# Two-layer graph attention on 64 graphs: softmax by pairs of graphs, division ahead of the transposes, half groups at both ends

## What is computed

```python
nx = ln(x, ln1_g, ln1_b)
q, k, v = nx @ wq + bq, nx @ wk + bk, nx @ wv + bv      # 8 heads of 32
bias = where(adj > 0, 0.1 * adj * adj, -inf)
x1 = x + softmax(q @ k.T / sqrt(32) + bias) @ v @ wo + bo
x = x1 + gelu(ln(x1, ln2_g, ln2_b) @ w1 + b1) @ w2 + b2
w = softmax(where(adj == 0, -inf, (x @ Wq) @ (x @ Wk).T / 16))
out = layer_norm(x + w @ (x @ Wv) @ Wo + bo1, gamma, beta)
```

## Time and profile before

| | us |
|---|---|
| median of 3 runs (range) | 1021.38 (1020.01 to 1025.15) |
| the profiled execution | 1021.12 |
| its span, first to last instruction | 1019.0 |
| mean granted TensorE clock | 0.981 |
| PE, DVE, ACT, POOL busy | 959.4, 616.8, 644.4, 409.3 |

### The profile page before, as it was taken

The page is one execution under the profiler, slowest core; times in us unless marked ns, Lnnn a source line. Parts: engine busy times, 40 slices in busy tenths (PEclk is TensorE's granted clock), DMA queues, the critical chain, the costliest instruction groups (busy, mean ns, idle before and its releaser), DMA issues.

```text
span 1019.0 us, 22667 instructions
## 1 busy us (share of the span) xinstructions
PE 959.4 (94%) x7512; PEld 827.0 (81%) x7512; DVE 616.8 (61%) x2460; ACT 644.4 (63%) x1890; POOL 409.3 (40%) x310
## 2 busy tenths in 40 slices
PE   4877999999999999999999999999999999999894
PEld 4755988888898888879888888989888888988783
DVE  3445567485756658575665758476674857565554
ACT  2536658576765768576665857676585767656552
POOL 3214245253444535344443525344452534442322
PEclk9868999999999999999999999999999999999998
DMA  7001001000100001000000100010010001000000
GB/s 232 22 1 32 2 12 42 12 21 21 31 21 31 21 10 41 10 21 21 31 21 10 41 10 21 21 31 21 11 41 10 21 21 31 21 1 21 2 22 21
DMA packets 32557, 26.20 MB, mean 26 GB/s; under 512 B 3984, under 2 KB 32272, under 8 KB 32528
## 3 DMA queue, kind: packets, MB, share of 16 engines
q1 hardware_dynamic: 29584, 25.83, 7.7%
q10 hardware_dynamic: 2944, 0.01, 0.2%
HBM read 17.44 MB, written 8.39 MB: 25 GB/s over the span
## 4 chain that ended last, share of the span: by engine, by line
PE 81%; DVE 7%; issue 2%; ACT 1%; POOL 0%; DVEq 0%; POOLq 0%
PE bank L255 21%; PE bank L256 18%; PE bank L257 18%; PE bank L368 5%; PE bank L392 5%; PE bank L385 3%; PE bank L359 3%; PE bank L472 3%; DVE p_s L952 2%; DVE nx L926 2%; DVE y L1043 1%; PE bank L374 1%; PE bank L324 1%; PE bank L437 1%; ACT p_s L691 0%
## 5 line engine op out<-in xcount | busy, mean ns | idle before, releaser
L691 ACT ACTIVATE p_s<-p_s,neg_max 128x128 f32<-128x128 f32 x512 | 197.9, 390 | 86.4 <-DVE neg_max L952 86.4
L255 PE MATMUL bank<-w_hi,hT_hi 128*128 128x256 f32 x512 | 150.1, 293 | 0.0
L257 PE MATMUL bank<-w_hi,hT_lo 128*128 128x256 f32 x512 | 143.8, 281 | 0.0
L256 PE MATMUL bank<-w_lo,hT_hi 128*128 128x256 f32 x512 | 143.7, 281 | 0.0
L952 DVE CUSTOM_DVE_ANT_0 p_s<-bank,bias 128x128 f32<-128x128 f32 x512 | 113.0, 285 | 47.2 <-PE bank L359 47.2
L1267 POOL COPY rwide<-rsum 128x256 f32<-128x256 f32 x64 | 25.4, 397 | 252.8 <-DVE rsum L965 252.8
L255 PE MATMUL bank<-n2T_hi,w_hi 128*128 128x512 f32 x256 | 108.7, 425 | 1.9 <-DVE n2T_lo L855 1.9
L255 PEld LDWEIGHTS bank<-w_hi,hT_hi 128*128 128x128 f32 x512 | 96.3, 188 | 5.9 <-issue 3.0
L257 PE MATMUL bank<-n2T_hi,w_lo 128*128 128x512 f32 x256 | 100.9, 394 | 0.0
L256 PE MATMUL bank<-n2T_lo,w_hi 128*128 128x512 f32 x256 | 100.9, 394 | 0.0
L714 ACT ACTIVATE bank<-bank,b_c 128x512 f32<-128x512 f32 x128 | 84.4, 660 | 24.0 <-PE bank L257 21.6
(11 more groups left out here) (159 smaller groups left out, 2420.3 us busy)
## 6 DMA issues: line engine op xcount, KB each, us to landing
xs<-in_x SPq DMA_DIRECT2D x16, 512.0 KB, 3.5
out<-y SPq DMA_DIRECT2D x15, 512.0 KB, 2.9
adj_i<-in_adj SPq DMA_DIRECT2D x16, 256.0 KB, 2.7
w_raw<-in_L_gnn_w SPq DMA_DIRECT2D x1, 1024.0 KB, 10.4
y<-in_L_gnn_w SPq DMA_DIRECT2D x1, 512.0 KB, 8.3
vo<-in_L_gnn_w SPq DMA_DIRECT2D x1, 512.0 KB, 9.3
out<-y SPq DMA_DIRECT2D x2, 256.0 KB, 2.1
x<-in_L_gnn_wk SPq DMA_DIRECT2D x1, 256.0 KB, 6.0
```

Of the source, the lines that this page charges most:

```text
L255: mm(out, a_hi, b_hi, start=first, stop=False)
L256: mm(out, a_hi, b_lo, start=False, stop=False)
L257: return mm(out, a_lo, b_hi, start=False, stop=last)
L691: last = run(p_s[:, h, :], p_s[:, h, :], ACT.Exp, scale=-1.0, bias=neg_max[:, b % 2, h:h + 1], accum_out=psum[:, b % 2, h:h + 1])
```

## The change

There are 17 groups now: 15 of four graphs, the first and the last of two (`size`, `pair0`, `graph0`, `ln0` give sizes and counts). Attention of layer 0 goes by pairs of graphs. `scores`, `attend` and `out_project` do both graphs in one go; of a pair, row block `r` of the four holds two graphs by two heads. `exps` writes to the PSUM bank the scores came from. `divided` on DVE takes the inverse of the sums and multiplies from PSUM into `p_s` ahead of the transposes. So `widen`, `rsum_transpose`, `rT_copy` and their tiles go, and `normalise` becomes a copy (`attn_copy`). `p_transpose` writes back into the four banks, and each of ACT and DVE copies two of them.

```diff
-            def scores(g, b):
-                if b == 0:
+            def scores(g, q):
+
+                if q == 0:
                     pe.wait_ge(act_k, 2 * g + 2)
                     pe.wait_ge(act_q, 2 * g + 2)
-                pe.wait_ge(dve_x1, 4 * g + b)
-                for t in range(KT):
+                pe.wait_ge(dve_x1, pair0(g) + q)
+                for place in range(4):
+                    b, t = 2 * q + place // 2, place % 2
                     for r in range(HPT):
-                        rows_r = slice(HD * r, HD * r + HD)
-                        last = mm(bank[r][:, nodes(t)], qT[rows_r, t, nodes(b)], kT[rows_r, t, nodes(b)],
+                        part = slice(HD * r, HD * r + HD)
+                        last = mm(bank[r][:, nodes(place)], qT[part, t, nodes(b)], kT[part, t, nodes(b)],
                                   start=True, stop=True, tile_position=(HD * r, 0))
                 last.then_inc(pe_s, 1)
 
...
+            def p_transpose(g, q):
+                for r in range(HPT):
+                    pe.wait_ge(dve_p, 4 * (pair0(g) + q) + r + 1)
+                    for place in range(4):
+                        last = tr(bank[r][:, nodes(place)], p_s[:, r, place, :], ident[:, :])
+                    last.then_inc(pe_pT, 1)
+
+            def attend(g, q):
+
+                pe.wait_ge(act_pT, 2 * (pair0(g) + q) + 2)
+                pe.wait_ge(dve_pT, 2 * (pair0(g) + q) + 2)
+                pe.wait_ge(act_v, pair0(g) + q + 1)
+                for place in range(4):
+                    b, t = 2 * q + place // 2, place % 2
                     for r in range(HPT):
-                        last = mm(av_area[HD * r:HD * r + HD, nodes(t)], v[:, b, HPT * t + r, :],
-                                  pT[:, HPT * t + r, :], start=True, stop=True, tile_position=(0, HD * r))
+                        last = mm(bank[av_bank][HD * r:HD * r + HD, nodes(place)], v[:, b, HPT * t + r, :],
+                                  pT[:, r, place, :], start=True, stop=True, tile_position=(0, HD * r))
                 last.then_inc(pe_av, 1)
...
+            def out_project(g, q):
+                pe.wait_ge(dve_attn, pair0(g) + q + 1)
+                for b in range(2):
+                    for t in range(KT):
+                        last = mm(bank[wo_bank][:, row(b)], avT[:, 2 * b + t, :], wo_f[:, t, :],
+                                  start=(t == 0), stop=(t == KT - 1))
                 last.then_inc(pe_wo, 1)
...
-            def p_transpose(g, b):
-                pe.wait_ge(dve_s, 8 * g + 2 * b + 2)
-                for h in range(HEADS):
-                    if h % HPT == 0:
-                        pe.wait_ge(act_p, 8 * g + 2 * b + h // HPT + 1)
-                    last = tr(bank[p_bank[h // HPT]][:, nodes(h % HPT)], p_s[:, h, :], ident[:, :])
-                last.then_inc(pe_pT, 1)
-
-            def rsum_transpose(g, b):
-                pe.wait_ge(pool_rwide, 4 * g + b + 1)
-                for t in range(KT):
-                    last = tr(rT_area[:, nodes(t)], rwide[:, HPT * t:HPT * t + HPT, :].rearrange("p h d -> p (h d)"),
-                              ident[:, :])
-                last.then_inc(pe_rT, 1)
-
...
+            def exps(g, q, r):
+
+                act.wait_ge(dve_s, 4 * (pair0(g) + q) + r + 1)
+                for place in range(4):
+                    last = run(bank[r][:, NODES * place:NODES * place + NODES], p_s[:, r, place, :], ACT.Exp, scale=-1.0,
+                               bias=neg_max[:, r, place:place + 1], accum_out=psum[:, r, place:place + 1])
+                last.then_inc(act_p, 1)
+
+            def pT_copy(g, q, r):
+                act.wait_ge(pe_pT, 4 * (pair0(g) + q) + r + 1)
+                run(pT[:, r, :, :], bank[r][:, :].rearrange("p (h n) -> p h n", h=4), ACT.Identity).then_inc(act_pT, 1)
...
+            def divided(g, q, r):
+                count = 4 * (pair0(g) + q) + r + 1
+                dve.wait_ge(act_p, count)
+                V.reciprocal(rsum[:, r, :], psum[:, r, :]).then_inc(dve_r, 1)
+                dve.wait_ge(dve_r, count)
+                V.tensor_tensor(p_s[:, r, :, :], bank[r][:, :].rearrange("p (h n) -> p h n", h=4),
+                                rsum[:, r, :, None].to_broadcast([128, 4, NODES]), ALU.mult).then_inc(dve_p, 1)
+
+            def pT_copy(g, q, r):
+                dve.wait_ge(pe_pT, 4 * (pair0(g) + q) + r + 1)
+                V.tensor_copy(pT[:, r, :, :], bank[r][:, :].rearrange("p (h n) -> p h n", h=4)).then_inc(dve_pT, 1)
+
+            def attn_copy(g, q):
+                dve.wait_ge(pe_av, pair0(g) + q + 1)
+                V.tensor_copy(avT[:, :, :], bank[av_bank][:, :].rearrange("p (h n) -> p h n", h=4)).then_inc(dve_attn, 1)
+
```

The opening: the vectors are loaded as rows of 128 and transposed by one PE instruction (`vector_columns`), w1 (in two DMAs) and w2 come after the weights of layer 1 and the broadcast rows, and ACT and DVE make the parts of w2 at the end of the first turn (`high_w2` ahead of the exponentials of group 1, `low_w2` last on DVE):

```diff
+            sp.dma_start(x_bo[:, 0:2, :], group_of(x, "n d", 0)).then_inc(x_bo_load, 16)
+            load_weight("wo", wo_f[:, :, :], wo)
+            for n, src in (("wq1", wq1), ("wk1", wk1), ("wv1", wv1), ("wo1", wo1)):
+                sp.dma_start(raw[n], src.rearrange("(t p) n -> p t n", p=128)).then_inc(w_load["l1"], 16)
             for dst, src in row_loads:
                 sp.dma_start(dst[:, :], src.rearrange("(a d) -> a d", a=1).to_broadcast([128, D])).then_inc(row_load, 16)
-            for g in range(1, 4):
+            for t in range(KT):
+                sp.dma_start(w1_raw[t], w1[128 * t:128 * t + 128]).then_inc(w_load["w1"], 16)
+            load_x(1)
+            for i in range(2):
+                load_weight("w2", w2_raw[i], w2[HIDDEN // 2 * i:HIDDEN // 2 * (i + 1)])
+            load_adj(1)
+            for g in range(2, 4):
                 load_adj(g)
                 load_x(g)
             store(0)
-            with sp.Fori(4, GROUPS) as g:
+            with sp.Fori(4, GROUPS - 1) as g:
                 load_adj(g)
                 load_x(g)
                 store(g - 3)
-            for g in range(GROUPS - 3, GROUPS - 1):
+            load_adj(GROUPS - 1)
...
+            dve.wait_ge(pe_cols, 1)
+            V.tensor_copy(vec_cols[:, :], bank[4][:, 0:COLS]).then_inc(dve_cols, 1)
             sums1(0)
             moments(1, 0)
-            dve.wait_ge(ln1_load, LN1_ALL)
-            V.tensor_scalar(ln1_gs[:, :], cols["ln1_g"][:, :], SCALE0, None, ALU.mult).then_inc(dve_shift, 1)
-            norm1(0, first=True)
+            dve.wait_ge(dve_cols, 1)
+            V.tensor_scalar(ln1_gs[:, :], cols["ln1_g"], SCALE0, None, ALU.mult).then_inc(dve_shift, 1)
+            norm1(0)
             low_weight("wk", wk_p, cols["ln1_g"])
-            shifts_kq()
-            shift_v()
             nxT_low(0)
             low_weight("wq", wq_p, ln1_gs)
+            shifts_kq()
             low_weight("wv", wv_p, cols["ln1_g"])
-            biased(0, 0)
+            shift_v()
+            for r in range(HPT):
+                biased(0, 0, r)
+            for r in range(HPT):
+                divided(0, 0, r)
             turn(1, 0, None, None)
```

More of the change, by code:

```diff
@@ L389, in out_project @@
-            def out_project(g, b):
-                pe.wait_ge(dve_attn, 4 * g + b + 1)
-                for t in range(KT):
-                    last = mm(wo_area, avT[:, t, :], wo_f[:, t, :], start=(t == 0), stop=(t == KT - 1))
-                last.then_inc(pe_wo, 1)
-            def n2_transpose(g):
-                pe.wait_ge(ln_dve[2], LN_STEPS * g + LN_STEPS)
-                for t in range(KT):
-                    for b in range(PER):
+            def p_transpose(g, q):
[4 more added lines that the diff above has]
+                    last.then_inc(pe_pT, 1)
@@ L412, in mlp_up, with mlp_down @@
                 for t in range(KT):
[L413 removed]
+                    last = mm3(bank[up_bank[j % 4]][:, toks(g)], both(w1_p, ALL, t, nodes(j)), both(n2T, ALL, t, toks(g)),
                                t == 0, t == KT - 1)
                 last.then_inc(pe_up, 1)
[L417 to L418 removed]
+            def mlp_down(g, q):
+                if q == 0:
@@ L419, in mlp_down @@
                     pe.wait_ge(dve_h, HT * g + 5)
-                if b >= 2 and steps[0] == 0:
-                    pe.wait_ge(dve_x2, 4 * g + b - 1)
-                for j in steps:
-                    if b == 0:
-                        pe.wait_ge(dve_h, HT * g + j + 1)
-                    last = mm3(bank[down_bank[b]][:, 0:D], both(hT, ALL, j, nodes(b)), both(w2_p, ALL, j),
-                               j == 0, j == HT - 1)
-                if steps[-1] == HT - 1:
-                    last.then_inc(pe_down, 1)
@@ L431, in x2_transpose @@
-            def x2_transpose(g, P):
-                if P:
-                    pe.wait_ge(dve_nxT, 2 * g + 6)
-                pe.wait_ge(dve_x2, 4 * g + 4)
+                for b in (2 * q, 2 * q + 1):
+                    for j in range(HT):
+                        if b == 0:
+                            pe.wait_ge(dve_h, HT * g + j + 1)
+                        last = mm3(bank[down_bank[q]][:, row(b)], both(hT, ALL, j, nodes(b)), both(w2_p, ALL, j),
```

(19 more changed lines are left out.)

958 lines of the change are left out of this document (446 added, 512 removed).

## The result

The changed kernel takes 982.77 us (median of 4 runs, 979.88 to 983.18), the kernel before 1023.05 in the same runs: a ratio of 0.9589, 95% interval 0.9559 to 0.9619. The forecast was 986.0 with a range of 967 to 1007. The profiled span is 980.7 where 984.0 was forecast; the four executions had spans of 978.1 to 981.4.

The account below looks back on a forecast made before the run. PE, busy 94% of the span, was taken as the bound: a turn is its list plus its waits. 114 + 13 x 57.0 + 53 + 76 = 984.0 of span, plus 2.1, gave 986 us, range 967 to 1007.

Parts of the forecast that it names:

- group 1's MLP starts: Opening: first MLP at 64.4, then a turn of 50 with half a group in the MLP, so 114 us.
- 13 steady turns: Turns between full groups: 57.0 us each against 58.57 before, from PE's instructions of 55.6 plus waits of 0.6 and 0.8.
- turn with half a group in P: Near the end: 57.0 less 4.7 for the shorter part, plus 0.7 at norm 2, so 53 us.
- last two turns: The end: 104.4 us before, less 16.6 and 7 for two fewer graphs, with smaller corrections, gives 76.
- PE's list: Steady turn: PE's instructions without new waits take 55.6 us, after 2.94 of savings on transposes, products, scores, projection and a wait.
- the wait for `y`: Steady turn: v's wait for layer 1, 0.62 us, disappears because y is about 1.0 us old or older at its new places.
- The two new waits: Steady turn: PE waits 0.6 us ahead of pair 0's out_project for the avT copy, 0.8 ahead of norm 2's transposes for nx.
- second rival: Steady turn: DVE is later, low parts 1 and 7 also become waits, 1.5 us a turn more, 1006; chance 0.15.
- The slacks: Steady turn: the probabilities are ready before PE wants them, by 1.7 us for pair 0 and 3.2 for pair 1.
- fourth rival: Probabilities' chain becomes the bound if each exponential to PSUM costs x more; at 0.72 each, 1045 us; chance 0.05.
- The opening: Start of kernel: first k at 14.7 us (bounds 14.2 and 19.68), first scores 21.8, first MLP 64.4, then a 50 turn.
- third rival: Half-group turns run at 1.2 GHz: 10 to 12 us more at the opening, 5 at the end, 1002; chance 0.12.

Follow-up runs that it names:

- the run without waits: Changed kernel with norm 2 ahead of the copy of tT, norm 1's sums behind the copy to avT, low part 7 directly behind low part 6: span 958.8 us.

## Why the prediction held, step by step

The sum was 984.0 and the span 980.7. By its terms:

| | forecast | measured | |
|---|---|---|---|
| group 1's MLP starts | 114 | 109.8 | -4.2 |
| 13 steady turns | 741.0 | 737.9 | -3.1 |
| turn with half a group in P | 53 | 54.15 | +1.15 |
| last two turns | 76 | 78.9 | +2.9 |

The terms miss by -7.3 and +4.05, so that the span came out within 3.3 is in part luck. The cause that the forecast gives for a steady turn, PE's list and two named waits, is what the runs show. That for the opening is not.

- **PE's list.** 55.6 forecast, 55.17 measured in the run without waits; the waits, 1.4 forecast, are worth 1.57 there, so the two misses partly cancel in the turn's 56.74. The product with v was put at 1.20 a pair and measures 1.21 (0.09 of start ahead of it, 1.02, and 0.10 in the six matmuls behind), the scores at 1.20 and measure 1.20, the output projection at 1.80 and measures 1.84, the transposes of the probabilities at 1.75 and measure 1.74. The row of the trace for a 128-column transpose (0.11) was right: four took 0.41. The Trainium skill, "TensorE: Matmul & The Clock Gate", section "Back-to-back issue gap", has the forecast's 56 ns as the gap of an isolated matmul and about 81 ns for a sustained stream; both are below the 0.10 to 0.11 of this trace. The difference of 0.4 lies mostly in the transposes of the two norms' rows: by the distance of starts they take 1.58 a turn in the run without waits and took 2.53 before, 0.95 less, where the sum had only the wait for `y`, 0.62.
- **The two new waits.** 0.6 and 0.8 forecast, 0.56 and 0.84 measured at their places, both with the cause that the forecast named. The experiments add that the cures differ. Norm 2's wait was an order on DVE with idle time beside it and fell with one exchange. That of `out_project` came back at low part 7, whose slack of about 0 the forecast had as its second rival; it went only when that part was moved as well.
- **The slacks.** Pair 1's probabilities: 3.2 forecast, 3.15 measured (477.68 to 480.83). Pair 0's: 1.7 and 1.77 (454.57 to 456.34). These decided against the fourth rival. Its price x was zero. (By its own formulas an exponential of 0.72 makes the two pairs 4.3 late together and not 4.6; and half of the 1.24 for the removed transposes is 8 in 13 turns and not 7. Nothing else hangs on either.)
- **The opening.** Too long by 4.2, and 1.7 of it is the first k: 14.7 forecast, 13.0 measured. Even the lower bound of 14.2 was too high: it was PE's first free time before, with eight transposes of `nx` ahead of it (1.74) where a group of two has four (0.88). First scores came at 19.7 (21.8), the first MLP at 60.4 (64.4). The turn behind took 49.4 against 50, but of other parts: PE's waits there were 2.6 for v, behind ACT's exponentials, 1.9 for the low part behind w2, 1.1 in four for the probabilities, and 0.5 at norm 2, where the forecast had 4, 3 and 2; and the clock read 1.00, where it had 2 for the lower level. That this term came out is luck.
- **What the opening's gain is made of** was told wrongly. The forecast's sum line put it to a group of two filling the pipeline sooner. Sixteen full groups lose only 3.8; the vectors' load is worth 6.1 of the span (7.3 at the first MLP), each by one profiled execution. If the two add up, the remaining 5 of the ends' 14.7 were not separated (order by pairs, order of the loads, w2's parts).
- **The turn with half a group in P.** Too short by 1.15. The forecast shortened P and put norm 2's wait up by 0.7, as it came (1.46 against 0.69). It left out that a shorter P uncovers two more waits, 0.8 for the transposed probabilities of layer 1 and 0.59 for x2's low part, which no steady turn has; the one ahead of `out_project` is gone.
- **The end.** Too short by 2.9. The forecast had PE idle for 3 at x2's transposes and the clock as a rival of its own, with 5 at the end. The wait of 2.58 came, and the clock fell behind it: 2.2 in the projection with Wq Wk. The third rival, of the clock, was true in this place and not in the opening, where the clock's mean was 0.89 against 0.84 before.

## To carry to other kernels

Where PE is the bound and each engine has a list by hand, count what stands ahead of the one result that PE wants, on the engine that makes it: the step of 0.7 that waits for PE itself belongs behind the one that doesn't. Having removed a wait, look at what had a slack smaller than that wait, since it is the next one; move both or neither. And a change of several parts is worth taking apart even when its sum came out: here the vectors' load, eight small DMAs, gave more than the new sizes of groups (5.4 or more of the span against 3 to 4). When a part of a turn is made shorter, ask which waits it used to cover. And where one execution is compared with one other, look at the clock of each stretch first: the last stretch of the same instructions took 32.4 and 35.2.

## What was not expected of the hardware

DVE's multiply by the inverses lasts 691 to 693 ns in every one of its 128 executions when one operand comes from PSUM. With both in SBUF (the run with exponentials to SBUF) its mean is 854, and the single ones tell why. POOL's and DVE's rows of that run:

```profile
475.73 1.50 POOL L1220 TENSOR_SCALAR adj_s<-adj_g 128x512 f32<-128x512 f32 x1
477.32 1.53 POOL L1222 TENSOR_TENSOR adj_s<-adj_s,adj_g 128x512 f32<-128x512 f32 x1
```

```profile
475.84 1.04 DVE L947 TENSOR_TENSOR p_s<-p_s,rsum 128x512 f32<-128x512 f32 x1
...
477.01 0.69 DVE L947 TENSOR_TENSOR p_s<-p_s,rsum 128x512 f32<-128x512 f32 x1
...
477.82 1.57 DVE L947 TENSOR_TENSOR p_s<-p_s,rsum 128x512 f32<-128x512 f32 x1
```

The one of 1.57 begins inside POOL's multiply and ends 0.54 after it, somewhat less than its own length of 0.69. The one beside a POOL operation with one tensor input (1.04) ends before that does. The one of 0.69 starts ahead of POOL's multiply, which then takes 1.53, where the same one takes 1.29 in the changed kernel. All 72 multiplies without a POOL instruction beside them take 0.69. The Trainium skill, "SBUF — State Buffer", section "SBUF: two separate sides", says that the two engines share a pair of SBUF ports, and that a DVE operation with two SBUF inputs (beside a POOL operation that reads SBUF) or the POOL operation, whichever starts first, holds it for its whole length. The trace agrees within 0.15 beside POOL's multiply. Beside the operation with one input it doesn't: by the rule the multiply that starts at 475.84 could only begin at 477.23, and it had ended by 476.88. Why is open. So writing the exponentials to PSUM does have a use that the forecast didn't see: it keeps DVE out of POOL's way, 21 us of DVE's time in all (109.3 against 88.5), hidden here.

A wait costs PE more than its bracket: 0.69 idle cost 0.84 at its place and 0.90 a turn when removed, 0.40 cost 0.56. A bracket counts from the end of the matmul ahead, which is 0.39 long, while the next starts after 0.23 when nothing is waited for; the matmul behind a wait doesn't overlap the one ahead, and that is the 0.16.
